# Fourier-feature embedding: the single-block groups as split products too in the first three images, and the first rounding step of six groups on ScalarE

## The reference

```
xb   = 2.0 * pi * xyz[..., None] * freq_bands       # xyz (4, 3, 512, 192), 6 bands
feat = concatenate([sin(xb), cos(xb)], axis=-1)
h    = einsum('bnf,of->bno', feat.reshape(b, n, -1), W)   # 6912 features -> 192
```

## Time and profile before

| | us |
|---|---|
| median of 3 runs | 993.57 |
| the runs | 992.65 to 998.92 |
| span of the profiled execution | 993.9 |
| embedding: first matmul to the end of the last native matmul | 10.1 to 294.9 |
| first native matmul of image 1 / 2 | 88.22 / 156.86 |

### The profile page before, as it was taken

The page is one execution under the profiler, slowest core; times in us unless marked ns, Lnnn a source line. Parts: engine busy times, 40 slices in busy tenths (PEclk is TensorE's granted clock), DMA queues, the critical chain, the costliest instruction groups (busy, mean ns, idle before and its releaser), DMA issues. The chain is left out here.

```text
span 993.9 us, 20032 instructions
## 1 busy us (share of the span) xinstructions
PE 890.0 (90%) x6459; PEld 787.2 (79%) x6459; DVE 728.3 (73%) x1703; ACT 647.6 (65%) x1218; POOL 141.7 (14%) x204
## 2 busy tenths in 40 slices
PE   5999999999998789898989898899699996799996
PEld 5899999999986577667766776676498875799995
DVE  6899979979944597569757965787567335687785
ACT  4765857757824597669767975897554321876862
POOL 1000000000001043304430432144400000000000
PEclk9999999999997899999999999999889999699998
DMA  8003110169931597259715961697210021442201
GB/s 274 22 23 99 38 33 0 37 105 139 138 58 41 154 278 233 59 155 285 221 51 172 291 202 47 196 273 214 66 43 1 14 84 32 134 147 91 78 2 63
DMA packets 83801, 114.11 MB, mean 115 GB/s; under 512 B 12271, under 2 KB 44476, under 8 KB 83724
## 3 DMA queue, kind: packets, MB, share of 16 engines
q1 hardware_dynamic: 82636, 112.39, 41.8%
q10 hardware_dynamic: 1088, 0.79, 0.2%
HBM read 62.31 MB, written 47.67 MB: 111 GB/s over the span
## 5 line engine op out<-in xcount | busy, mean ns | idle before, releaser
L427 PE MATMUL psum<-w,feat 128*128 128x192 f32 x912 | 160.3, 331 | 13.9 <-ACT feat L357 10.1
L427 PEld LDWEIGHTS psum<-w,feat 128*128 128x128 f32 x912 | 149.1, 192 | 14.7 <-issue 11.4
L656 POOL TENSOR_SCALAR a_scores<-a_scores,a_inv 112x514 f32<-112x514 f32 (+1 forms) x160 | 112.6, 705 | 269.5 <-DVE a_inv L1028 269.2
L1013 DVE CUSTOM_DVE_ANT_0 a_scores<-psum,a_bias 112x514 f32<-112x514 f32 (+1 forms) x160 | 110.0, 688 | 46.2 <-PE psum L732 37.7
L885 ACT ACTIVATE a_scores<-a_scores,a_least 112x514 f32<-112x514 f32 (+1 forms) x160 | 116.7, 729 | 9.8 <-DVE a_least L1013 9.2
L745 PE MATMUL psum<-ident,a_scores 112*112 112x112 f32 (+1 forms) x800 | 99.4, 255 | 19.8 <-DVE a_probsT L1023 14.5
L445 PE MATMUL psum<-w_parts,parts 128*128 128x384 f32 x368 | 112.8, 371 | 3.3 <-DVE parts L232 2.8
L357 ACT ACTIVATE feat<-turn 128x1024 f32<-128x1024 f32 (+1 forms) x60 | 58.4, 974 | 85.2 <-DVE turn L215 53.9
L745 PEld LDWEIGHTS psum<-ident,a_scores 112*112 112x112 f32 (+1 forms) x800 | 74.7, 133 | 41.7 <-issue 19.7
L732 PE MATMUL psum<-a_kh,a_q 128*112 128x258 f32 (+1 forms) x320 | 99.1, 331 | 1.0 <-DVE a_least L1013 1.0
L447 PE MATMUL psum<-w_parts,parts 128*128 128x192 f32 x384 | 96.5, 251 | 0.0
(11 more groups left out here) (298 smaller groups left out, 1819.0 us busy)
## 6 DMA issues: line engine op xcount, KB each, us to landing
shear<-a_pos SPq DMA_DIRECT2D x128, 224.9 KB, 3.9
a_bias<-shear SPq DMA_DIRECT2D x128, 224.4 KB, 3.9
shear<-zero SPq DMA_DIRECT2D x20, 448.9 KB, 18.1
e_fc<-in_e_fc_dram SPq DMA_DIRECT2D x16, 384.0 KB, 3.9
x<-in_xT_dram SPq DMA_DIRECT2D x20, 256.0 KB, 3.0
e_proj<-in_e_proj_dram SPq DMA_DIRECT2D x8, 576.0 KB, 5.6
shear<-a_pos SPq DMA_DIRECT2D x32, 130.5 KB
a_bias<-shear SPq DMA_DIRECT2D x32, 130.3 KB
```

Of the source, the lines that this page charges most:

```text
L427: mm = pe.matmul(sums[m][:, 0:D], feat[:, r, j, 0, 128 * m:128 * m + 128], w[:, k, :], start=begins, stop=ends)
L656: pool.tensor_scalar(row, row, inv[0:TILES[g % NT][1], g % TT:g % TT + 1], 1.0, ALU.mult, ALU.mult).then_inc(weighed, 1)
L1013: dve.tensor_tensor_reduce(halves(scores[0:r, g % TT, 0:PADL]), psum2(score_pair(g), r), halves(bias[0:r, g % MR, :]), -1.0 / 8, BIG, ALU. ...
```

## The change

Three things, all in `embed_phase`:

1. In images 0, 1 and 2 the singles too are multiplied in split terms alone, with no native matmuls. ACT's `first_parts` and DVE's `rest` run for groups 12 to 14 as well, and in image 0 the weights of the singles are split. In image 3 the singles stay native. DVE's remainder of group g-1 stands in step g as before; for group 14, the last, it stands behind step 14, ahead of step 0 of the next image.
2. The `shift` of groups 6 to 11 (channel blocks 2 and 3) is made by ACT in all images, as an Identity activation with a scale and a bias from memory. It stands at the head of ACT's group g-2.
3. ACT's image 3 is written out behind its loop. `w_parts` grows from 12 to 15 groups, and the program sets a smaller scratch for dynamic DMA.

```diff
+BY_SCALAR = range(BANDS, 2 * BANDS)
...
 def whole(b, g):
     n, r = GROUPS[g][1], g % NF
-    dve.wait_ge(shifted, b * NE + g + 1)
+    if g in BY_SCALAR:
+        dve.wait_ge(shifted_a, b * NSA + shifts_a(g))
+    else:
+        dve.wait_ge(shifted_d, b * (NE - NSA) + g + 1 - shifts_a(g))
...
 def image(b, first=False, more=True):           # DVE
...
         if g + 2 < NE:
-            shift(b, g + 2, first)
+            if g + 2 not in BY_SCALAR:
+                shift(b, g + 2, first)
...
         absolute(b, g)
-        if g - 1 in pairs:
+        if g >= 1 and (more or g - 1 in pairs):
             rest(b, g - 1)
-        if first and g in pairs:
+        if first:
             split_weights(g)
...
+    if more:
+        rest(b, NE - 1)
...
+def shift(b, g, first):                         # ACT
...
+    act.wait_ge(cos_done, b * NE + g - NF + 1)
...
+    act.activation(near[:, r, 0:n, :], x[:, c0:c0 + n, :], ACT.Identity, bias=magic[:, :],
+                   scale=freq[:, u:u + 1]).then_inc(shifted_a, 1)
+
 def group(b, g, first):
     n, r = GROUPS[g][1], g % NF
+    if g + 2 in BY_SCALAR:
+        shift(b, g + 2, first)
     act.wait_ge(turn_done, b * NE + g + 1)
...
-    if g in pairs:
+    if more or g in pairs:
         first_parts(b, g)
...
-mm = native(0)                                  # PE
-mm = native(1)
 if n == 2:
-    mm = split()
+    native(0)
+    native(1)
+mm = split()
```

More of the change, by code:

```diff
@@ L55 @@
 NE = len(GROUPS)
+BY_SCALAR = range(BANDS, 2 * BANDS)
+NSA = len(BY_SCALAR)
 NU = len(UNITS)
@@ L77, in embed_phase @@
     consts_set, edges_set = sem("consts_set"), sem("edges_set")
-    shifted, rounded, turn_done, aturn_done = sem("shifted"), sem("rounded"), sem("turn_done"), sem("aturn_done")
+    shifted_a, shifted_d, rounded, turn_done, aturn_done = (
+        sem("shifted_a"), sem("shifted_d"), sem("rounded"), sem("turn_done"), sem("aturn_done"))
+    shifts_a = lambda g: sum(e in BY_SCALAR for e in range(g + 1))
     sin_done, cos_done, feat_free, passed = sem("sin_done"), sem("cos_done"), sem("feat_free"), sem("turns_passed")
@@ L96, in embed_phase @@
         raw = s.place.rearrange("p (g j n) -> p g j n", g=NPAIR, j=2)
+        raw_of = lambda g: raw[:, g] if g in pairs else w[:, 2 * g:2 * g + 2, :]
         feat = sb("feat", [128, NF, 2, 2, N])
-        w_parts = sb("w_parts", [128, NPAIR, 2, 2, D], F32R)
+        w_parts = sb("w_parts", [128, NE, 2, 2, D], F32R)
         parts = sb("parts", [128, NF, 2, 2, N], F32R)
@@ L106, in embed_phase @@
         roots, inv = sb("roots", [128, 2, 4]), sb("inv", [128, 2, 4])
-        half_pi, eps = sb("half_pi", [128, 1]), sb("eps", [128, 2])
+        half_pi, eps, magic = sb("half_pi", [128, 1]), sb("eps", [128, 2]), sb("magic", [128, 1])
         freq = sb("freq", [128, NU])
@@ L153, in _ @@
                 if b == 1:
-                    sp.wait_ge(w_lo, NPAIR)
+                    sp.wait_ge(w_lo, NE)
                     for dst, src in ((s.wq, "a_wq"), (s.wk, "a_wk"), (s.wv, "a_wv"), (s.wo, "a_wo"), (s.m_w2, "m_w2"), (s.m_w1, "m_w1"),
@@ L190, in _ @@
             dve.memset(eps[:, 1:2], EPS * EPS).then_inc(consts_set, 1)
+            dve.memset(magic[:, :], MAGIC).then_inc(consts_set, 1)
             def shift(b, g, first):
@@ L201, in shift @@
                     stand_alone(dve, passed)
-                dve.tensor_scalar(near[:, r, 0:n, :], x[:, c0:c0 + n, :], freq[:, u:u + 1], MAGIC, ALU.mult, ALU.add).then_inc(shifted, 1)
+                dve.tensor_scalar(near[:, r, 0:n, :], x[:, c0:c0 + n, :], freq[:, u:u + 1], MAGIC, ALU.mult, ALU.add).then_inc(shifted_d, 1)
             def whole(b, g):
                 n, r = GROUPS[g][1], g % NF
-                dve.wait_ge(shifted, b * NE + g + 1)
+                if g in BY_SCALAR:
+                    dve.wait_ge(shifted_a, b * NSA + shifts_a(g))
+                else:
+                    dve.wait_ge(shifted_d, b * (NE - NSA) + g + 1 - shifts_a(g))
                 dve.tensor_scalar(near[:, r, 0:n, :], near[:, r, 0:n, :], MAGIC, None, ALU.subtract).then_inc(rounded, 1)
@@ L225, in split_weights @@
                 dve.wait_ge(w_hi, g + 1)
-                dve.tensor_tensor(w_parts[:, g, :, 1, :], raw[:, g], w_parts[:, g, :, 0, :].bitcast(F32),
+                dve.tensor_tensor(w_parts[:, g, :, 1, :], raw_of(g), w_parts[:, g, :, 0, :].bitcast(F32),
                                   ALU.subtract).then_inc(w_lo, 1)
@@ L230, in rest @@
                 r = g % NF
-                dve.wait_ge(hi_done, b * NPAIR + g + 1)
-                dve.tensor_tensor(parts[:, r, 1], feat[:, r, :, 1, :], parts[:, r, 0].bitcast(F32), ALU.subtract).then_inc(lo_done, 1)
+                dve.wait_ge(hi_done, b * NE + g + 1)
+                dve.tensor_tensor(parts[:, r, 1], feat[:, r, :, GROUPS[g][1] - 1, :], parts[:, r, 0].bitcast(F32), ALU.subtract).then_inc(lo_done, 1)
             def take_sums(i):
@@ L351, in _ @@
         def _(act):
+            def shift(b, g, first):
+                c0, n, f = GROUPS[g]
+                u, r = first_unit[g], g % NF
+                if f == 0:
+                    for c in range(c0, c0 + n):
+                        act.wait_ge(x_in[c], b * 16 + 16)
+                act.wait_ge(cos_done, b * NE + g - NF + 1)
+                if not first:
+                    stand_alone(act, passed)
+                act.activation(near[:, r, 0:n, :], x[:, c0:c0 + n, :], ACT.Identity, bias=magic[:, :],
+                               scale=freq[:, u:u + 1]).then_inc(shifted_a, 1)
             def group(b, g, first):
                 n, r = GROUPS[g][1], g % NF
+                if g + 2 in BY_SCALAR:
+                    shift(b, g + 2, first)
                 act.wait_ge(turn_done, b * NE + g + 1)
@@ L362, in split_weights @@
             def split_weights(g):
-                act.wait_ge(raw_in[g], 16)
-                act.copy(w_parts[:, g, :, 0, :], raw[:, g]).then_inc(w_hi, 1)
+                act.wait_ge(raw_in[g] if g in pairs else w_in[g], 16)
+                act.copy(w_parts[:, g, :, 0, :], raw_of(g)).then_inc(w_hi, 1)
             def first_parts(b, g):
@@ L369, in first_parts @@
                 act.wait_ge(cos_done, b * NE + g + 1)
-                act.copy(parts[:, r, 0], feat[:, r, :, 1, :]).then_inc(hi_done, 1)
+                act.copy(parts[:, r, 0], feat[:, r, :, GROUPS[g][1] - 1, :]).then_inc(hi_done, 1)
             def take_roots(i):
@@ L383, in take_h1 @@
                                    scale=norm1[:, c:c + 1]).then_inc(h1_out, 1)
-            act.wait_ge(consts_set, 3)
+            act.wait_ge(consts_set, 4)
             act.sem_inc(rooted, 1)
@@ L394, in _, with image @@
                 group(0, g, True)
-                if g in pairs:
-                    split_weights(g)
-                    first_parts(0, g)
-            with act.Fori(1, B) as b:
+                split_weights(g)
+                first_parts(0, g)
+            def image(b, more):
                 for g in range(NE):
                     group(b, g, False)
-                    if g in pairs:
+                    if more or g in pairs:
                         first_parts(b, g)
@@ L406, in _ @@
                         take_h1(b - 1)
+            with act.Fori(1, B - 1) as b:
+                image(b, True)
+            image(B - 1, False)
             take_roots(B - 1)
@@ L422, in native @@
                     for m in range(4):
-                        ends = g == NE - 1 and j == 1
                         begins = g == j == 0
@@ L427, in native @@
                         mm = pe.matmul(sums[m][:, 0:D], feat[:, r, j, 0, 128 * m:128 * m + 128], w[:, k, :],
-                                       start=begins, stop=ends)
-                        if ends:
-                            mm.then_inc(sums_done, 1)
+                                       start=begins, stop=False)
                     return mm
@@ L435, in split @@
                         pe.wait_ge(w_lo, g + 1)
-                    pe.wait_ge(hi_done, b * NPAIR + g + 1)
-                    pe.wait_ge(lo_done, b * NPAIR + g + 1)
+                    pe.wait_ge(hi_done, b * NE + g + 1)
+                    pe.wait_ge(lo_done, b * NE + g + 1)
                     for j in range(2):
@@ L446, in split @@
                                           start=False, stop=False)
-                            mm = pe.matmul(sums[m][:, 0:D], f(1), w_parts[:, g, j, 0, :], start=False, stop=False)
-                    return mm
-                mm = native(0)
-                mm = native(1)
+                            ends = g == NE - 1 and j == 1
+                            mm = pe.matmul(sums[m][:, 0:D], f(1), w_parts[:, g, j, 0, :], start=False, stop=ends)
+                            if ends:
+                                mm.then_inc(sums_done, 1)
+                    return mm
                 if n == 2:
-                    mm = split()
+                    native(0)
+                    native(1)
+                mm = split()
                 if g < NE - 1:
```

(2 more changed lines are left out.)

## The result

| | before | with the change |
|---|---|---|
| median, us | 996.11 (4 runs) | 1022.72 (4 runs) |
| profiled span, us | 993.9 | 1019.7 |
| last addition of the embedding, us | 295.36 | 314.24 |
| span behind it, us | 698.5 | 705.5 |

The ratio is 1.022 (95% interval 1.0166 to 1.0274); one disturbed run of the four, 1260.7 us, is left out of it but not out of the median, and the other three took 1013.8, 1021.5 and 1023.9 us. The forecast was 1012.5, range 1004 to 1018: the direction holds, the time lies above the range.

What follows compares the result with a forecast made beforehand. The prediction took PE to bound the embedding's body, with a loop between DVE and ACT pacing image 0. Seams of 4.8 + 3.6 + 3.6 = 12.0 us plus 6.9 of clock on 993.9 gave 1012.5 us, range 1004 to 1018.

Steps and rivals of the forecast that it cites:

- Pair groups bound by PE, DVE just in time at the seams: Embedding: PE full in image 1's body, 4.87 us a pair group; DVE's idle time between images leaves it only just in time.
- First seam, +4.8 us: End of image 0: DVE's three weight splits and three remainders 4.83 us, ACT's last cast 0.3, pair groups -0.35.
- Seams behind images 1 and 2, 3.6 + 2.3 each with the clock of the seam before: Group 14's remainder waits for ACT's cast, making `take_sums` 3.6 us later; PE's slower restart costs 2.3 us per seam.
- the last clock term: Start of image 3: PE's lower clock after idling at the third seam, 2.3 us.
- The clock, +6.9: PE idles at all three seams and returns at a lower clock, 2.3 us each; bounds 5.4 and 13.5 us.
- The moved shift is worth nothing outside image 0: Bodies of images 1 to 3: DVE is not the bound, and ACT's idle time covers its 24 added activations.
- its -0.35 in image 0: Image 0's pair groups: five save 0.27 us each, 1.35 in all; group 6 adds 1.0 on ACT.
- The sum "on a span of 993.9, which is 0.3 above the median of the runs": Whole kernel: 12.0 us of seams and 6.9 of clock, 18.9 us, added to the profiled span, giving 1012.5 us.
- the upper bound of my own terms, 1019: Whole kernel: upper end of the forecast with seams and clock, 1011 to 1019 us by the clock's bounds, chance 0.75.
- PE's saving: Singles on PE: DVE's added work fits its idle time at the seam, 2.65 us less, 990.9 us; chance 0.05.
- ACT did not become the bound: Pair groups: a shift of 1.8 us on ACT would add 0.3 us in 18 groups, 1018 us; chance 0.05.
- the seams without the clock: Seams between images: the waits come as computed but PE's granted clock stays, 1005.6 us; chance 0.12.

Runs made afterwards that it cites:

- filled seams: The changed kernel with 15 more unread fp32 matmuls on PE at each of the three seams between images; ratio 1.0144, embedding's end at 308.08 us.

## Why the prediction was right and wrong

- *Pair groups bound by PE, DVE just in time at the seams*: right. The remainder of group 14, with the next image's steps queued behind it, stands in the rows of the seam behind image 1, and the third wait of PE, 5.65 us, repeats it behind image 2.
- *First seam, +4.8 us*: image 1's first matmul moved from 88.22 to 93.65, 5.4 us. The term is 0.6 short, in the singles: from the row that the sum starts at, 71.60 in the earlier trace rows, to the next image's first step DVE needed 7.90 us before and needs 13.64 now, 5.74 more, where the sum had 5.13.

```profile
71.28 0.42 DVE L216 TENSOR_SCALAR near<-near 128x512 f32<-128x512 f32 x1
84.92 0.69 DVE L216 TENSOR_SCALAR near<-near 128x1024 f32<-128x1024 f32 x1 [0.23 <-DVE h1T L353]
```

- *Seams behind images 1 and 2, 3.6 + 2.3 each with the clock of the seam before*: the first matmuls of images 1, 2 and 3 stood at 88.22, 156.86 and 225.58 and now stand at 93.65, 167.59 and 242.19. The periods grew from 68.64 to 73.94 and from 68.72 to 74.60: by 5.3 and 5.9, against 5.9 forecast. From image 3's first matmul to the embedding's end it is 72.05 us for 69.78, 2.3 more, the last clock term. So 5.4 + 5.3 + 5.9 + 2.3 = 18.9 us. The first period is 0.6 short because its clock term is 1.7 us (73.94 less the 72.22 of the filled seams) and not 2.3; that this and the 0.6 of the first seam cancel is luck.
- *The clock, +6.9*: 6.2 to 6.7 by the filled seams. Right in size. The Trainium skill ("TensorE: Matmul & The Clock Gate", section "What's actually happening") puts the ramp under 1% of a typical span; the trace agrees, 6.7 of 993.9 us is 0.7%, but to leave it out would have lost a third of the embedding's loss.
- *The moved shift is worth nothing outside image 0*: right by the version with the shift only; its -0.35 in image 0 is too small to be told from the 0.3 us between profiles of one kernel, and its price on ACT, 1.24 us instead of 1.06, stayed under cover.
- *The sum "on a span of 993.9, which is 0.3 above the median of the runs"*: this is the step that failed. It took all that lies behind the embedding as a constant, 698.5 us, and so put the movement of the untouched stages at nothing. Ten profiles of seven kernels, which have the same work there, gave 694.7 (the filled seams) to 710.1, and the median of before was 996.7 over 17 runs later and 1000.2 over 17 more. Of the 10.2 us between 1012.5 and 1022.7, 6.9 are this: 705.5 us behind the embedding for 698.5. Another 2.1 are the base's figure: in the runs that have both, the time is 1.8 us above the profiled span (1021.5 for 1019.7), so the span of 993.9 does not belong to the median of 993.57, 0.3 below it, but to a run of some 995.7. The other 1.2 lie between the middle run, 1021.5, which is the profiled one, and the median of four. On the base of the first 17 the same sum gives 1015.6, where the changed kernel's median beside them was 1018.8. As a share the sum is 18.9/993.9 = 1.9%, inside the interval of the measured ratio (1.66 to 2.74%). The range, 1004 to 1018, stopped 1 us short of the upper bound of my own terms, 1019, and had nothing in it for the 11.6 us between two profiles of one kernel in its untouched stages.
- *The rivals*: PE's saving did not decide; ACT did not become the bound; the seams without the clock are what the filled seams look like.

What stays open: why the clock falls in the second layer in one run and not in the next. The rows show that it does at the same instructions; no run here isolated a cause. That the change adds time behind the embedding is not shown: the mean of the three profiles of before is 703.7 us, of the changed kernel's two 703.6. The medians still differ by 22 to 27 us, some us more than the 18.9 to 19.5 of the embedding; few profiles can't settle these.

## What to carry to other kernels

An instruction that waits for another engine holds up all that its own engine has listed behind it. So count everything behind such a wait, up to the next point where the busiest engine needs a result, before the place of the instruction is chosen. When the busiest engine goes idle, price its lower clock on the return as well: here it was a third of the embedding's loss. And before a forecast of one or two per cent, look how much the untouched stages move between runs of the same kernel, and put that into the range.

## What the runs showed that I had not expected

Idle times of 0.3 to 1.7 us at the seams were followed by full clock in all kernels here but one, where the clock had fallen 5 us earlier behind 3.10 us; one of 2.74 us was followed by the lower clock. The falls are not tied to long idle times alone: in the second layer the clock fell behind one of 1.13 us in one profile of the kernel before and stayed full behind the same one in another, and in the changed kernel it fell once with no idle time ahead. Adding 15 useless matmuls at each seam took 6.2 to 6.7 us off the changed kernel's embedding.
